# A graph layer with picked and fetched source rows: ten and eleven picks in turn, rounds merged together, base reads moved, distances ahead of a wait

## The reference

```python
def _nnconv(x, src, dst, edge_attr, ew, eb, rw, rb):
    W = (edge_attr @ ew + eb).reshape(edge_attr.shape[0], x.shape[1], rw.shape[1])
    xj = x[src]
    msg = jnp.einsum('ei,eio->eo', xj, W)
    agg = jax.ops.segment_sum(msg, dst, num_segments=x.shape[0])
    return agg + x @ rw + rb
```

## Time and profile before

| | us |
|---|---|
| median of 3 runs (7298.59 to 7299.79) | 7299.14 |
| the profiled execution's own time | 7314.06 |
| its span | 7312.0 |
| PE busy (matmuls) | 6839.5 |
| PEld busy (weight loads) | 5832.2 |
| DVE busy | 6244.8 |
| POOL busy | 5336.2 |
| ACT busy | 4982.5 |

### The profile page before, as it was taken

One profiled execution on the slowest core, in us unless ns is written; L12 is line 12 of the kernel. 1 busy time (PEld: TensorE's weight loads), 2 busy tenths in 40 slices (PEclk: granted clock), 3 DMA queues, 4 the chain that ended last, 5 costly groups with the idle time before them and its releaser, 6 DMA issues.

```text
span 7312.0 us, 131050 instructions
## 1 busy us (share of the span) xinstructions
PE 6839.5 (94%) x49442; PEld 5832.2 (80%) x49442; DVE 6244.8 (85%) x7568; ACT 4982.5 (68%) x8367; POOL 5336.2 (73%) x5635
## 2 busy tenths in 40 slices
PE   4999999999999899999999999989999999999998
PEld 3888888888888688888888888868888788888887
DVE  5888888888888788888888888878888888888885
ACT  4767676777776577766766666657767666766665
POOL 4777777777777577777777777757777777777774
PEclk7999999999999899999999999989999999999997
DMA  6111111111111111111111111111111111111111
GB/s 46 32 32 32 32 32 32 32 32 32 32 29 32 29 32 32 32 32 32 29 32 32 31 30 32 32 29 32 32 32 31 30 32 32 30 31 32 32 29 23
DMA packets 714221, 229.54 MB, mean 31 GB/s; under 512 B 573057, under 2 KB 664593, under 8 KB 713593
## 3 DMA queue, kind: packets, MB, share of 16 engines
q1 hardware_dynamic: 493253, 172.63, 10.6%
q0 software_dynamic: 180000, 46.44, 6.5%
q10 hardware_dynamic: 40340, 2.08, 0.7%
HBM read 217.19 MB, written 3.52 MB: 30 GB/s over the span
## 4 chain that ended last, share of the span: by engine, by line
POOL 63%; issue 22%; PE 10%; DVE 4%; DMA 0%; ACT 0%; DVEq 0%; POOLq 0%; ACTq 0%; SPq 0%
POOL xg L516 63%; PE bank L1151 7%; DVE xbig L704 1%; DVE xg L765 1%; PE bank L1220 1%; PE bank L1232 1%; PE bank L1118 1%; DVE spread L760 1%; DVE agg L658 0%; DVEq L798 0%; ACT agg L932 0%; DMA xbig<-in_x 0%; POOLq L379 0%; DVE agg L803 0%; PE bank L1164 0%
## 5 line engine op out<-in xcount | busy, mean ns | idle before, releaser
L516 POOL DMA_INDIRECT xg<-node_table,idx x5625 | 5335.4, 949 | 1902.2 <-issue 1711.4
L1151 PE MATMUL bank<-nodes,low_hot 128*128 128x448 f32 x26250 | 5738.0, 374 | 197.9 <-DVE spread L760 158.3
L1151 PEld LDWEIGHTS bank<-nodes,low_hot 128*128 128x128 f32 x26250 | 4904.8, 190 | 864.3 <-DVE spread L760 285.6
L990 ACT ACTIVATE distance<-key_all,low_id 128x640 bf16<-128x640 int16 x3000 | 2242.5, 818 | 1817.4 <-issue 1182.3
L760 DVE TENSOR_TENSOR spread<-mask,bank 128x448 f32<-128x448 uint8 x3750 | 2157.9, 615 | 642.8 <-PE bank L1151 616.0
L996 ACT ACTIVATE low_hot<-distance,one 128x640 fp32r<-128x640 bf16 x3000 | 2233.3, 817 | 0.0
L765 DVE TENSOR_REDUCE xg<-spread 128x80 f32<-128x2240 f32 x750 | 1864.6, 2486 | 25.7
L704 DVE TENSOR_TENSOR xbig<-xg,bank 128x1280 f32<-128x1280 f32 x750 | 1338.4, 1811 | 143.4 <-DMA xg<-node_table,idx 141.1
L1118 PE MATMUL bank<-xbig,rows_room 128*32 128x144 f32 x12450 | 569.7, 290 | 0.0
L1118 PEld LDWEIGHTS bank<-xbig,rows_room 128*32 128x32 f32 x12450 | 457.6, 110 | 78.3 <-issue 76.1
L1118 PE MATMUL bank<-xbig,hot 128*32 128x144 f32 x6300 | 351.7, 288 | 0.0
(11 more groups left out here) (118 smaller groups left out, 1349.8 us busy)
## 6 DMA issues: line engine op xcount, KB each, us to landing
key_all<-edge_keys SPq DMA_DIRECT2D x375, 320.0 KB, 3.6
xg<-node_table,idx POOLq DMA_INDIRECT x5625
ea<-in_edge_attr SPq DMA_DIRECT2D x375, 100.0 KB
idx<-in_src SPq DMA_DIRECT2D x375, 7.5 KB
node_table<-rows_room SPq DMA_DIRECT2D x3, 781.2 KB
xbig<-node_table SPq DMA_DIRECT2D x3, 672.0 KB
xbig<-in_x SPq DMA_DIRECT2D x2, 781.2 KB
xbig<-in_src ACTq DMA_DIRECT2D x1, 937.5 KB
```

The costliest lines, as they stand in the source:

```text
L516: pool.indirect_dma_start(out=xg[u][:, j, :], out_offset=None, in_=table[:, :], in_offset=bass.IndirectOffsetOnAxis(ap=idx[u][:, j:j + 1], ...
L990: nc.scalar.activation(distance[f][:, 0:tiles.stop - tiles.start, :], key[u % KEYS][:, tiles, :], ACT.Abs, bias=low_id[:, f:f + 1]).then_i ...
L1151: last = nc.tensor.matmul(p_sel[place_in_all % BANKS], low_hot[:, i // 2, t, :], nodes[:, i, :, :].rearrange("p d f -> p (d f)"), start=i ...
```

## The change

- `PICKS` is `(10, 11)`: even groups have ten picked and fifteen fetched tiles, odd groups eleven and fourteen. In all 186 tiles (62 per layer) go from POOL's gathers to picks. A first half has five or six picks, a second half five.
- PE transposes all rounds of a group together (`transpose_rounds`), when the loop over picks is at `t == 3` (behind three picks of a group of ten, four of a group of eleven), where they stood behind the second and the fourth pick. The two results of two rounds lie in different columns of bank 2, so the second doesn't wait for the first one's copy. The waits of all rounds stand ahead of the first. The messages are sent at `t == 8` instead of 7.
- DVE reads the bases of the additions earlier: three between the product of the picked tiles and that of the fetched ones, two behind the latter, where all five stood right ahead of the additions.
- ACT computes the distances of a half, and the copies that stand between them and the ReLUs, ahead of the wait for the picks that still use the old one-hots; the copies of transposed rounds move in between the distances and the ReLUs of the first half.

```diff
-PICKS = (10,)
+PICKS = (10, 11)
+MERGE_AT = 3
+SEND_AT = 8
...
-        p_zT, p_zxT = bank[2][:, 0:SPAN], bank[2][0:D, SPAN:2 * SPAN]
+        p_zT = [bank[2][:, i * 2 * SPAN:i * 2 * SPAN + SPAN] for i in range(PAIR)]
+        p_zxT = [bank[2][0:D, i * 2 * SPAN + SPAN:(i + 1) * 2 * SPAN] for i in range(PAIR)]
...
+                        ended = quad_rounds((g - 1) // QUAD) if g and ends_quad(g - 1) else range(0)
+                        under_picked = (len(ended) + 1) // 2
                         multiply_picked(layer, b, u)
+                        bases = read_bases(ended[:under_picked])
                         multiply_fetched(layer, b, u)
+                        bases += read_bases(ended[under_picked:])
                         set_merges(layer, g)
...
-                            add_quad(layer, (g - 1) // QUAD)
-                add_quad(layer, QUADS - 1)
+                            add_quad(layer, (g - 1) // QUAD, bases)
+                add_quad(layer, QUADS - 1, read_bases(quad_rounds(QUADS - 1)))
...
-                if k:
-                    act.wait_ge(s_pick, picks_before(k - 1) + parts((k - 1) % G)[half].stop - first_pick((k - 1) % G))
-
-
                 before = k * (4 * FOLD) + half * 2 * FOLD
                 act.wait_ge(s_dist, before + 1)
                 for f in range(FOLD):
                     nc.scalar.activation(distance[f][:, 0:tiles.stop - tiles.start, :], key[u % KEYS][:, tiles, :], ACT.Abs,
                                          bias=low_id[:, f:f + 1]).then_inc(s_dist, 1)
                 if between is not None:
-                    copy_rounds(layer, between)
+                    between()
+                if k:
+                    act.wait_ge(s_pick, picks_before(k - 1) + parts((k - 1) % G)[half].stop - first_pick((k - 1) % G))
...
+            def transpose_rounds(layer, rounds):
+
+                if rounds:
+                    n, after = layer * R + rounds[0], layer * R + rounds[-1] + 1
+                    pe.wait_ge(s_z, after)
+                    if n:
+                        pe.wait_ge(s_zT, n)
+                    pe.wait_ge(s_add, layer * R + rounds[-1] - rounds[-1] % QROUNDS + CREDIT)
+                for r in rounds:
+                    transpose_round(layer, r)
...
-                            if t in (1, 3) and t // 2 < len(ended):
-                                transpose_round(layer, ended[t // 2])
-                            if t == 7 and ended and ends_quad(g - 1):
+                            if t == MERGE_AT:
+                                transpose_rounds(layer, ended)
+                            if t == SEND_AT and ended and ends_quad(g - 1):
                                 messages_of(layer, (g - 1) // QUAD)
```

## The result

The changed kernel takes 7434.78 us (median of 4 runs, 7432.26 to 7441.6), the kernel before 7299.47 beside it: a ratio of 1.0187, with a 95% interval of 1.0171 to 1.0202. The profiled executions took 7433.57 and 7314.06, so the trace has 119.5 us to explain.

What follows compares the result with a forecast made beforehand. The loop of PE and DVE was taken as the bound, hardly faster than POOL. 265.1 - 92 - 44 - 16 + 1 = +114 us gave 7428 on the profiled execution, 7413 against the median; range 7320 to 7475.

Steps and rivals of the forecast that it cites:

- What bounds the kernel: Whole loop: PE and DVE take 72.90 us a quad, hardly faster than POOL's 75.2; DVE delays the fifth pick's bank.
- The extra picks: PE's picks in each layer's loop: 186 more at 1.425 us each, nothing hiding them, +265.1 us.
- merged rounds: PE's transposes in interval A: one break in the picks in place of two, -16 us.
- The gathers removed: POOL's gathers: 58 a quad, under the loop, so products stop waiting for them, -92 us.
- Bases read early: DVE ahead of the additions: its idling there goes, -44 us; PE covers a later product in A.
- Nothing for B's transpose wait: PE in interval B: the transpose's 1.50 us wait goes, but the fifth pick's bank is late next, so nothing booked.
- the transpose's wait was on the path: Rival, interval B: the 1.50 us wait comes back as time too, giving +23 us, 7322; chance 10%.
- Distances ahead of the wait: ACT's one-hots made earlier: no row shows PE waiting for them, so zero.
- Before the layers: DVE ahead of the layers: seven instructions a tenth wider and a few small ones, +1 us, between 0 and 4.
- The clock: Slow intervals B, granted clock 0.91, 19.77 us against 19.13: number left as it is; 29 us up or down otherwise.
- The clock falls in every B: Rival, interval B: one longer idle piece of PE slows the clock each time, 7442 us; chance 13%.
- PE has room, POOL is the bound: Rival, whole loop: extra picks fit into PE's time and gathers set the pace, 233 us less, 7066; chance 8%.

Runs made afterwards that it cites:

- e6: The change with a fifth PSUM bank for picks, both rounds' sums sharing bank 0: 7233.07 us, ratio 0.991.
- e10: The kernel before with ten and eleven picks in turn, its transposes kept behind the second and fourth pick made: 7467.8 us, ratio 1.0231.
- e2: The change with ten picks in every group, so all the moves and no extra pick: 7310.11 us, ratio 0.9995.
- e3: The change with the five bases read right ahead of the additions again: 7517.48 us, ratio 1.0277.
- e4: The change with transposes at two places again, behind the second and fourth pick, each with its own waits: 7494.38 us, ratio 1.0245.
- e12: The change with the merged transposes one pick earlier, behind two picks of a group of ten: 7404.65 us, ratio 1.014.
- e1: The kernel before with ten and eleven picks in turn, which also put B's transpose behind one pick instead of two: 7618.41 us, ratio 1.0418.
- e5: The change with ACT's wait for the picks ahead of the distances again: 7417.57 us, ratio 1.0157.
- e7: The change with ten, eleven, eleven and eleven picks, so interval B has an eleventh too: 7657.62 us, ratio 1.0487.
- e11: The five-bank kernel with eleven picks in one group of three instead of one of two: 7163.14 us, ratio 0.9809.

## Why the prediction held, and where it was off

Step by step, in the prediction's order, with the sums of the table above.

- **What bounds the kernel.** Right: the loop of PE and DVE was hardly faster than POOL, so taking gathers from POOL could give back only its waits. The bank at the fifth pick was named as DVE's doing, and e6 shows that bound directly: with one more bank the idling in B goes and the kernel becomes 2.7% faster than the change.
- **The extra picks, +265, with the merged rounds, -16.** Together 249 were booked. Measured are 90 x (21.16 - 19.72) + 93 x (18.39 - 16.91) = 267. The picks' price held: without the moves (e10) it is 90 x (21.13 - 19.72) + 93 x (18.39 - 16.91) = 264.5. The **merged rounds were mis-sized**, about nothing in place of 16; e2, with merged rounds and no extra pick, has A's median at 19.72 as before. The sum by the Trainium skill's start-to-start time (TensorE: Matmul & The Clock Gate, "Wait — 56ns, not 53.3ns?") would have been 246 for the picks alone; the trace disagrees with it here as it did before.
- **The gathers removed, -92.** 75.5 us went from D's sum; C's and A's sums grew by 7.9 and 14.9 less than their medians would have it (129.7 against 93 x 1.48, 114.7 against 90 x 1.44), A's partly in the short intervals at the layers' ends. That makes 98 at most.
- **Bases read early, -44.** B at full clock lost 0.50, and e3, which puts the reads back, gets 0.51 of it back: 46 us for 93. The late product of A was seen as well (22.3 us over 94 times, on DVE), and PE is busy to the end of A, as booked.
- **Nothing for B's transpose wait.** Right where two picks or more stand ahead of the transpose: e4 and e12 have the wait and the change has not, and all have a B of 18.63 or 18.64. In e1, with one pick ahead, the rival's mechanism holds and the wait costs time. The rival "the transpose's wait was on the path" falls for the change itself.
- **Distances ahead of the wait, 0.** Nothing gained, as booked; a loss of up to 0.3% is open (e5).
- **Before the layers, +1.** The first sum starts 2.5 us later.
- **The clock, number and price left as they were.** Both were wrong, and by luck they cancel. The prediction read 15 slow B of 31 in layer 0 and took 46 of 93; the view gives 14 and 37. Slow B fell from 37 to 13 of 93, and one costs 1.54 us where it cost 0.65: 20 us against 24. The price rose because of where the wait lies. In a slow B before, PE was busy for 18.28 instead of 16.99 and idle for 1.49 instead of 2.14: half of the longer work took the place of idling. In the change's rows above, busy time goes from 16.90 to 18.34 and idling stays at 1.82 and 1.81: nothing is absorbed. "The clock falls in every B" did not happen here, but in e7 it nearly did.

So +113 was booked for the loops (the sum without what lies before the layers), and 267 - 98 - 57 = +112 was measured. That these agree to 1 us is luck as well: picks and merging cost 18 more than was booked, while the gathers gave 6 more and B 13 more (-57 for -44, of which the reads are 46 and the clock's change some 4; the rest was not traced). The missing 22 us of the forecast lie elsewhere: 7 ahead of, between and behind the loops, of which one was booked, and 15 by which the profiled run of the kernel before stood above its median, while that of the change did not. The prediction subtracted those 15. They are no oddity of one run: on the chip of e1 to e4 the kernel before took 7313 to 7316 in 14 of 15 runs. Where they lie is not shown, as no run of it at 7300 was profiled; so of the 135 us between the medians the traces explain 120.

"PE has room, POOL is the bound" is refuted: products wait for no gather, and the picks cost all that they take. The rule on weight-load busy time (the Trainium skill, Perfetto Trace Analysis, "Identifying the Most-Contended Engine") would have left PE room at 80%; the trace disagrees. One sign was named wrongly: POOL's new idling ends with edge attributes landing, hardly ever with PE's sums.

## What to carry to other kernels

Price moved work on the engine that holds each stretch, not by busy shares: here a pick cost all of its 1.43 us in intervals where PE or DVE's chain had no slack. The transposes' wait, moved out of the way, was worth nothing here, since PE met the same delay at the ring of buffers; what paid was the slot that was missing (a fifth bank: from 1.0187 to 0.991), and then a new balance of the engines (0.9809). And where a place is counted in a loop, as `t in (1, 3)` was, a change of the loop's bounds moves it: e1 paid 2% (151 us over e10) for one pick's difference.

## What the runs showed of the hardware

How PE idles in an interval B goes with its clock, within the kernels run here. The pieces of idling are medians over the B of one profiled run at full clock:

| kernel | PE's idling in B, us | slow B of 93 |
|---|---|---|
| e6, e11 | 0.50, 0.47 | 0, 0 |
| e4, e12 | 1.05 and 0.51 | 0, 0 |
| e10 | 1.47 and 0.61 | 21 |
| before | 1.50 and 0.64 | 37 |
| change, e5 | 1.82 | 13, 13 |
| e2 | 1.84 | 36 |
| e3 | 0.15 and 1.95 | 40 |
| e7 | 2.00 | 76 |
| e1 | 2.92 | 67 |

The kernels whose longest piece is 1.05 us or less have no slow B, and those with 1.47 or more all have some. Their sums, up to 1.56 and from 1.82, part them in the same way, so these runs do not tell whether the cutting or the sum matters, and neither orders the counts among the rest. In the change the idling is 1.82 in slow B and in the others alike, and slow B come back evenly for a while (in layer 0 of the kernel before in quads 2, 4, 6 and 8, counted from 0, in that of the change in quads 1, 6 and 11). So something besides the idling picks the one slow B among its neighbours; it was not found.

In a slow B the granted clock is 0.91 or 0.92, part of it at the lower of the two levels (0.50 between 1017.30 and 1020.50 us in the slow B of the change shown above). 1.5 to 1.6 us are lost where no later wait absorbs them, 0.65 to 0.74 in the two kernels (before, and e10) where the transposes stood behind the second and the fourth pick.
